# Residual, graph convolution and layer norm in one kernel: a shorter second pass, and the last rows shared and summed in another way

## The reference

```python
masks = (relation[None] == rel_ids[:, None, None, None]).astype(x.dtype)
h = jnp.einsum('rbnm,bmd->rbnd', masks, x)
y = jnp.einsum('rbnd,rdo->bno', h, weight)
x = _layernorm(x + y + bias, axis=-1)          # eps 1e-5
```

## Time and profile before

| | us |
|---|---|
| median of 3 runs (lowest, highest) | 120.71 (120.52, 120.75) |
| the profiled execution, its own time | 120.54 |
| span of the profiled execution, first to last instruction | 118.8 |
| PE busy (matmuls) | 106.6 |
| ACT, DVE, POOL busy | 88.1, 84.8, 70.3 |
| bytes moved | 42.22 MB, mean 355 GB/s |

### The profile page before, as it was taken

The page is one execution under the profiler, slowest core; times in us unless marked ns, Lnnn a source line. Parts: engine busy times, 40 slices in busy tenths (PEclk is TensorE's granted clock), DMA queues, the critical chain, the costliest instruction groups (busy, mean ns, idle before and its releaser), DMA issues.

```text
span 118.8 us, 2879 instructions
## 1 busy us (share of the span) xinstructions
PE 106.6 (90%) x1012; PEld 80.4 (68%) x1023; DVE 84.8 (71%) x252; ACT 88.1 (74%) x114; POOL 70.3 (59%) x132
## 2 busy tenths in 40 slices
PE   6788999899999979999999999999999999999400
PEld 2168898799997646767676767676868676679300
DVE  1055678397877848696959887787779777998840
ACT  4088277947797999799999499968987698925530
POOL 2007001940047998399569955995689577977740
PEclk9999999999999999999999999999999999999985
DMA  3999999999999999999999999999999999450271
GB/s 73 389 408 411 414 407 422 414 391 412 425 414 384 419 403 436 380 414 414 419 391 404 422 406 394 420 406 423 377 433 411 415 399 383 141 177 0 85 248 35
DMA packets 12419, 42.22 MB, mean 355 GB/s; under 512 B 882, under 2 KB 7155, under 8 KB 8947
## 3 DMA queue, kind: packets, MB, share of 16 engines
q1 hardware_dynamic: 12256, 41.49, 88.6%
q10 hardware_dynamic: 146, 0.52, 1.3%
HBM read 37.81 MB, written 4.19 MB: 354 GB/s over the span
## 4 chain that ended last, share of the span: by engine, by line
PE 58%; DMA 29%; SPq 5%; DVE 2%; issue 1%; ACT 0%; DVEq 0%
PE h_ps L619 32%; DMA adj_sb<-adj 29%; PE ids_t L601 16%; PE y_ps L633 9%; SPq L396 4%; PE ids_t L633 1%; DVE x_sb L758 0%; SPq L393 0%; SPq L412 0%; ACT std L539 0%; DVE stats L711 0%; DVE x_sb L705 0%; DVE moments L717 0%; DVEq L255 0%; DVE shift L751 0%
## 5 line engine op out<-in xcount | busy, mean ns | idle before, releaser
L522 ACT ACTIVATE junk<-adj_sb,minus 128x2048 bf16<-128x2048 int32 x32 | 63.8, 1994 | 0.4 <-DMA adj_sb<-adj 0.4
L699 DVE TENSOR_SCALAR mask_t<-ids_t 128x1024 bf16<-128x1024 uint16 x64 | 43.6, 687 | 25.2 <-PE ids_t L601 24.1
L601 PEld LDWEIGHTS ids_t<-ident,adj_sb 128*128 128x128 bf16 x512 | 36.5, 123 | 13.8 <-DMA adj_sb<-adj 2.7
L601 PE MATMUL ids_t<-ident,adj_sb 128*128 128x128 bf16 x512 | 40.0, 221 | 2.3 <-DMA adj_sb<-adj 2.2
L619 PE MATMUL h_ps<-mask_t,x_lo 128*128 128x512 bf16 (+2 forms) x184 | 33.5, 314 | 0.0
L619 PE MATMUL h_ps<-mask_t,x_hi 128*128 128x512 bf16 (+2 forms) x173 | 31.1, 310 | 1.2 <-DVE mask_t L699 0.6
L448 POOL TENSOR_TENSOR x_lo<-x_sb,x_hi 128x1024 f16<-128x1024 f32 x7 | 15.0, 2144 | 24.2 <-ACT x_hi L531 24.2
L488 POOL TENSOR_SCALAR x_sb<-x_sb,rstd,shift 128x128 f32<-128x128 f32 x55 | 24.0, 457 | 1.0
L535 ACT ACTIVATE h_all<-h_ps 128x512 f32<-128x512 f32 (+2 forms) x23 | 10.6, 463 | 18.1 <-PE h_ps L619 18.1
L454 POOL TENSOR_TENSOR x_sb<-x_sb,bias_sb 128x1024 f32<-128x1024 f32 x8 | 19.0, 2377 | 7.8 <-DVE x_lo L764 7.7
L619 PEld LDWEIGHTS h_ps<-mask_t,x_hi 128*128 128x128 f16 x184 | 15.6, 98 | 7.2 <-DVE mask_t L699 1.2
(11 more groups left out here) (44 smaller groups left out, 30.8 us busy)
## 6 DMA issues: line engine op xcount, KB each, us to landing
adj_sb<-adj SPq DMA_DIRECT2D x27, 1024.0 KB, 19.5
adj_sb<-adj SPq DMA_DIRECT2D x10, 512.0 KB, 8.4
x_sb<-x SPq DMA_DIRECT2D x7, 512.0 KB, 18.9
out<-x_sb SPq DMA_DIRECT2D x7, 512.0 KB, 16.7
x_sb<-x ACTq DMA_DIRECT2D x1, 512.0 KB, 5.4
out<-x_sb SPq DMA_DIRECT2D x2, 256.0 KB, 3.3
w_sb<-weight SPq DMA_DIRECT2D x1, 64.0 KB, 6.1
bias_row<-bias ACTq DMA_DIRECT2D x1, 0.5 KB
```

The costliest lines, as they stand in the source:

```text
L522: nc.scalar.activation(junk[:, at % 2], adj_sb[:, slot, 2 * k:2 * k + 2, :], ACT.Square, scale=2.0, bias=minus[:, 0:1], accum_out=squares[ ...
L601: last = nc.tensor.transpose(bank[:, j, :], words[:, j // step(b), j % step(b), 0, :], ident[:, :])
L699: nc.vector.tensor_scalar(mask_t[:, b % 2, :, u * P:(u + 1) * P], ids_t[u % T_BANKS][:, :, :].bitcast(UINT16), 1.0, None, ALU.mult).then_i ...
```

## The change

Four parts.

1. The second pass goes unit by unit instead of batch by batch, with x in fp32 instead of three bf16 parts. The code of one turn gets shorter on every engine; in PE's program it has 44 matmuls instead of 288.
2. PE adds the last unit's x: a matmul of x with an fp32 identity (`add_x`) opens the accumulation that `project(d)` closes. DVE has no sum for d any more: it takes statistics from PSUM and normalises from PSUM.
3. The found matmul stands ahead of `products(d)`, the write of `again` ahead of d's statistics, and `offer_guess(full)` ahead of `find_far`.
4. Rows at the end are shared anew: of full, POOL three and ACT five; of rb, POOL two, DVE two, ACT none. POOL and DVE normalise as (x - mean) * rstd. The shift is only made for full and ra, which ACT still normalises with it.

```diff
+        whole_ident = sb("whole_ident", [P, P], FP32)
...
         def second_pe(pe):
             pe.wait_ge(g_w, 16)
             with pe.Fori(0, B) as b:
...
+                with pe.Fori(0, J) as u:
+                    pe.wait_ge(g_cast, J * b + u + 1)
+                    for j in range(J):
+                        last = nc.tensor.transpose(ids_t[0][:, j, :], ids[:, j, :], ident[:, :])
+                    last.then_inc(g_tr, 1)
+                    pe.wait_ge(g_x, 16 * (b + 1))
+                    pe.wait_ge(g_mask, J * b + u + 1)
+                    for r in range(R):
                         for j in range(J):
+                            last = nc.tensor.matmul(h_ps[0][:, r * P:(r + 1) * P], x_sb[:, 0, j, :], masks[:, r, j, :],
+                                                    start=(j == 0), stop=(j == J - 1))
+                    last.then_inc(g_prod, 1)
+                    pe.wait_ge(g_h, J * b + u + 1)
                     for r in range(R):
+                        last = nc.tensor.matmul(y_ps[:, 0, :], h_all[:, 0, r * P:(r + 1) * P], w_sb[:, r, :],
+                                                start=(r == 0), stop=(r == R - 1))
                     last.then_inc(g_y, 1)
...
             def roots(r):
                 slot = r.b
+                shifted = r.index >= B - 2
...
+                if shifted:
+                    nc.gpsimd.tensor_scalar(minus_mean[:, r.index - (B - 2), r.us], mean[:, slot, r.us], -1.0, None,
+                                            ALU.mult).then_inc(s_minus, 1)
...
-                                        ALU.mult).then_inc(s_root, 1)
-                pool.wait_ge(s_root, r.index + 1)
-                nc.gpsimd.tensor_tensor(shift[:, slot, r.us], minus_mean[:, r.us], rstd[:, slot, r.us],
                                         ALU.mult).then_inc(s_rstd, 1)
+                if shifted:
+
+                    pool.wait_ge(s_rstd, r.index + 1)
+                    pool.wait_ge(s_minus, r.index - (B - 3))
+                    nc.gpsimd.tensor_tensor(shift[:, slot, r.us], minus_mean[:, r.index - (B - 2), r.us], rstd[:, slot, r.us],
+                                            ALU.mult).then_inc(s_shift, 1)
 
             def normalise(r, units):
...
-                    last = nc.gpsimd.tensor_scalar(rows[:, slot, u, :], rows[:, slot, u, :], rstd[:, slot, u:u + 1],
-                                                   shift[:, slot, u:u + 1], ALU.mult, ALU.add)
+                    last = nc.gpsimd.tensor_scalar(rows[:, slot, u, :], rows[:, slot, u, :], mean[:, slot, u:u + 1],
+                                                   rstd[:, slot, u:u + 1], ALU.subtract, ALU.mult)
...
-            normalise(full, full.units[:4])
+            normalise(full, full.units[:3])
             roots(ra)
             normalise(ra, ra.units[:2])
-            normalise(rb, rb.units[:1])
+            normalise(rb, rb.units[:2])
...
             copy_h(c)
-            normalise(full, full.units[4:5])
+            normalise(full, full.units[3:4])
             copy_h(e)
             root(ra)
-            normalise(full, full.units[5:7])
+            normalise(full, full.units[4:6])
             copy_h(d)
-            normalise(full, full.units[7:]).then_inc(s_aside, 1)
+            normalise(full, full.units[6:]).then_inc(s_aside, 1)
             root(rb)
             normalise(ra, ra.units[2:]).then_inc(s_aside, 1)
-            normalise(rb, rb.units[1:2]).then_inc(s_aside, 1)
...
+            def add_x(g):
+
+                pe.wait_ge(s_whole, 1)
+                pe.wait_ge(s_xb, g.b + 1)
+                nc.tensor.matmul(y_of(g)[:, 0, :], whole_ident[:, :], x_sb[:, g.b, g.first, :], start=True, stop=False)
...
             project(c)
-            products(d, 0, 1)
-            project(e)
             pe.wait_ge(s_found, 1)
             nc.tensor.matmul(ids_t[0][0:1, 0, 0:2].bitcast(FP32), found[:, :], ones[:, :],
                              start=True, stop=True).then_inc(s_count, 1)
+            products(d, 0, 1)
+            project(e)
+            add_x(d)
             project(d)
             second_pass(pe, second_pe)
...
+            def statistics_of_sum(g):
+
+                dve.wait_ge(s_y, g.index + 1)
+                nc.vector.bn_stats(stats[:, g.first, :], y_of(g)[:, 0, :]).then_inc(s_st, 1)
...
-                                               in1=guess[:, r.us], op0=ALU.add, op1=ALU.mult).then_inc(s_n[3], 1)
-
-            def shift_rows(r):
...
+                                               in1=guess[:, r.us], op0=ALU.add, op1=ALU.mult).then_inc(s_rstd_last, 1)
...
+            offer_guess(r)
             find_far()
             find()
-            offer_guess(r)
...
-            for g in (e, d):
-                sum_rows(g)
-                statistics(g)
-            combine(rb, d, range(J - 2, J))
+            sum_rows(e)
+            statistics(e)
             dve.wait_ge(s_count, 1)
             nc.vector.tensor_copy(again[:, :], ids_t[0][0:1, 0, 0:2].bitcast(FP32)).then_inc(s_again, 1)
-            for part in (invert, times_guess, times_guess_again, better_guess, shift_rows):
+            statistics_of_sum(d)
+            combine(rb, d, range(J - 2, J))
+            for part in (invert, times_guess, times_guess_again, better_guess):
                 part(rb)
-            normalise(rb, rb.units[2:])
+            normalise(rb, e.first, rows[:, rb.b, e.first, :])
+            normalise(rb, d.first, y_of(d)[:, 0, :]).then_inc(s_done, 1)
```

More of the change, by code:

```diff
@@ L266, in second_sp @@
                 sp.dma_start(x_sb[:, 0], x_v[b]).then_inc(g_x, 16)
-                for k in range(PAIRS):
-                    sp.dma_start(adj_sb[:, 0, 2 * k:2 * k + 2, :], adj_v[b, :, 2 * k:2 * k + 2, :]).then_inc(g_adj[k], 16)
-                for g in range(NG):
-                    sp.wait_ge(g_norm, NG * b + g + 1)
-                    sp.dma_start(out_v[b, :, g * GU:(g + 1) * GU, :], rows[:, 1, g * GU:(g + 1) * GU, :]).then_inc(g_out, 16)
-                sp.wait_ge(g_out, 16 * NG * (b + 1))
@@ L318, in second_pe @@
+                    last.then_inc(g_prod, 1)
+                    pe.wait_ge(g_h, J * b + u + 1)
                     for r in range(R):
-                        done = R * (NG * b + g) + r
-                        pe.wait_ge(g_mask, GU * (done + 1))
-                        if r >= 2:
-                            pe.wait_ge(g_h, done - 1)
-                        for j in range(J):
-                            for n, part in enumerate(parts):
-                                last = nc.tensor.matmul(
-                                    h_ps[r % 2][:, :], part[:, j, :], halves(masks[:, j, :], r % 2),
-                                    start=(j == 0 and n == 0), stop=(j == J - 1 and n == len(parts) - 1))
@@ new lines, in second_dve @@
+            with dve.Fori(0, B * J) as i:
+                dve.wait_ge(g_tr, i + 1)
+                for r in range(R):
+                    last = nc.vector.tensor_scalar(masks[:, r], ids_t[0][:, :, :], float(r + 1), None, ALU.is_equal)
+                last.then_inc(g_mask, 1)
+                dve.wait_ge(g_xb, i + 1)
+                dve.wait_ge(g_y, i + 1)
+                nc.vector.tensor_tensor(result, y_ps[:, 0, :], xb, ALU.add).then_inc(g_sum, 1)
+                dve.wait_ge(g_sum, i + 1)
+                nc.vector.bn_stats(stats[:, 0, :], result).then_inc(g_stats, 1)
+                dve.wait_ge(g_stats, i + 1)
+                nc.vector.memset(square[:, 0:1], 0.0)
+                nc.vector.bn_aggr(moments[:, 0, 0, :], stats[:, 0, :]).then_inc(g_var, 1)
+                dve.wait_ge(g_std, i + 1)
+                nc.vector.reciprocal(guess[:, 0:1], std[:, 0:1]).then_inc(g_root[0], 1)
+                dve.wait_ge(g_root[0], i + 1)
+                nc.vector.scalar_tensor_tensor(out=square[:, 0:1], in0=variance[:, 0, 0:1], scalar=EPS,
+                                               in1=guess[:, 0:1], op0=ALU.add, op1=ALU.mult).then_inc(g_root[1], 1)
+                dve.wait_ge(g_root[1], i + 1)
+                nc.vector.scalar_tensor_tensor(out=whole[:, 0:1], in0=square[:, 0:1], scalar=0.25,
+                                               in1=std[:, 0:1], op0=ALU.mult, op1=ALU.add).then_inc(g_root[2], 1)
+                dve.wait_ge(g_root[2], i + 1)
+                nc.vector.reciprocal(rstd[:, 0, 0:1], whole[:, 0:1]).then_inc(g_root[3], 1)
+                dve.wait_ge(g_root[3], i + 1)
+                nc.vector.tensor_scalar(result, result, mean[:, 0, 0:1], rstd[:, 0, 0:1],
+                                        ALU.subtract, ALU.mult).then_inc(g_norm, 1)
@@ L687, in _ @@
             s_worst = sem("worst_ready")
-            s_n = [sem(f"root{n}") for n in range(4)]
+            s_n = [sem(f"root{n}") for n in range(3)]
             def row_maxima(b):
@@ L746, in better_guess, with normalise @@
                 nc.vector.scalar_tensor_tensor(out=rstd[:, r.b, r.us], in0=twice[:, r.us], scalar=0.75,
[L747 to L760 removed]
```

(5 more changed lines are left out.)

153 lines of the change are left out of this document (38 added, 115 removed).

## The result

The changed kernel is slower: 122.69 us median of four runs, against 120.61 us for the kernel before beside it. The ratio is 1.0163, with a 95% interval of 1.0133 to 1.0193. I had forecast 119.9 us and a range of 119.1 to 120.6. The profiled execution took 122.76 us, its span 121.0. The ratios in this document are those of the comparison itself, not quotients of the medians; one run (one_input's of 123.80 us) was a slow one, and they leave it out.

What follows compares the result with a forecast made beforehand. PE was taken to bound the kernel up to 111.24 us, small row work to 114.21, then the last store, held by a code fetch. Last store -0.95 and POOL last +0.10 made -0.85 us: 119.9 us, range 119.1 to 120.6.

Steps and rivals of the forecast that it cites:

- Against it: both forms read one tile and two scalars: POOL's normalise: argument that the subtract form would not cost over 0.15 us a row more than the old mult/add.
- rival 3: POOL's two last rows, or add_x, cost more; end moves 0.3 to 0.4 us, 121.1 us without fetch gain; chance 0.08.
- the missing shift of sets 0 to 5: Two small POOL operations fewer per set, about 0.5 us, six times; no gain, since PE is the bound there.
- The term of -0.95 us for the last store: End of kernel: shorter jump and earlier flag let the last store land sooner, by 0.64 to 1.45 us, taken as 0.95.
- the jump is short but still starts the fetch of a block: PE's jump at the end: the block only comes earlier, by as much as the flag is read earlier, 0.64 us gained.
- worked out +0.10: Last rows: POOL replaces DVE as the last engine, ending at 114.31, 0.10 us later than the old end.
- My bound of 0.30 us lost: Last rows' worst case: add_x costs 0.47 us and POOL's rows slow to 0.52 us each.
- Rival 1: PE's jump still misses and takes 4 us again; only the earlier flag helps, 120.2 us; chance 0.14.
- Rival 2: Last store's stragglers aren't the fetch's doing and come anyway; only +0.10, 120.8 us, no difference; chance 0.12.

Runs made afterwards that it cites:

- one_input: Changed kernel with DVE's last two search operations written with one input tensor and one scalar column instead of two input tensors; 122.68 us, 1.0107 of before.
- forms: Kernel before with a different form of POOL's normalise (orders of subtract, mult, add) in each of sets 1 to 5; 120.46 us in one run.
- mult_add: Changed kernel with POOL's old normalise (multiply by rstd, add shift) for all sets but the last half's two rows; 120.68 us, 0.997 of before.
- add_mult: Changed kernel with POOL adding minus mean instead of subtracting mean, then multiplying by rstd; 120.64 us, 0.9983 of before.
- stub_pass: Kernel before with the change's second pass, PE's part cut to three matmuls a turn (not the reference's result); 119.28 us, 0.9866 of before.
- four_at_once: shared_as_before with the second pass's products on PE as 8 matmuls instead of 32; 119.05 us, 0.9866 of before.
- shared_as_before: Changed kernel with rows shared and shifted as in the kernel before, POOL using mult/add everywhere; 120.18 us, 0.9941 of before.
- short_pass: Kernel before with only the change's shorter second pass on all five engines; 120.78 us, 1.0007 of before.
- long_pass: shared_as_before with the long second pass of the kernel before; 120.07 us, 0.9928 of before.

## Why the prediction was wrong

- **"Against it: both forms read one tile and two scalars"** is the step that failed. I priced POOL's new rows at the old 0.44 to 0.52 us, and rival 3 had them cost something over 0.15 us more, worth 0.3 to 0.4 us, and only at the end. They cost 0.80 us, because the form has a subtract (forms). The error goes through the whole kernel: 55 rows at 0.35 us are 19 us of POOL's time, and POOL's last row ended at 118.28 us where I had worked out 114.31. I had called the missing shift of sets 0 to 5 "nothing" on the strength of a POOL busy 59%, but never asked what the new form did to the same sets. POOL then had 57.4 of 60 us to do and became the bound; with the subtract gone the loss went (mult_add 0.997, add_mult 0.998 of before). In the kernel before, DVE's two rows with this very form stood at 0.33 us, but no row of POOL did; that was the place for bounds on both sides, and the far one should have been that of an unknown operation, not that of the known one.
- **The term of -0.95 us for the last store** was mis-sized for this change. The reading behind it holds in its main point: a block of PE's code in front of the last store's packets costs 1.5 us by stub_pass, 1.1 us by four_at_once against shared_as_before. What it had wrong is whose block: with the short jump it isn't the one that PE jumps to and waits for. Of the two ways in which I let it go, the second happened: "the jump is short but still starts the fetch of a block". I priced it at 0.64 us, all that the flag is earlier. The block came even 1.05 us earlier, yet it gave 0.2 us in add_mult and nothing in short_pass, where the flag isn't moved. My step was that everything behind the block moves with it. But an earlier block stands before more packets: in shared_as_before it starts before any packet of ra's store, in add_mult after 100 of its 272, and the DMA engine that carries it still has the rest of both stores to do behind it. The packets that come one by one at the end (stub_pass) bear this out; no run took it apart. In the change itself the term came out at 1.8 us, for another reason: POOL's rows were so late that the block, fetched at 116.43 us, was through when the last store was issued at 118.31. That is luck for this term, paid for with the 4.07 us.
- **The rest of the working held.** With the subtract undone, flag, statistics, rstd and both engines' last rows came within 0.1 us of what was worked out, and POOL did take DVE's place as the last (+0.20 us against the old end, worked out +0.10). mult_add and add_mult show no cost of the PSUM source, the matmul with the identity or the new shares beyond that. My bound of 0.30 us lost was a little small: by its own terms it is 0.10 + 0.16 (add_x at 0.47 us, past the CAST's end) + 0.08 = 0.34 us.
- **Rival 1** (the jump still misses) fell: 371 ns. **Rival 2** (the stragglers aren't the fetch's doing) fell as an explanation, though its time, no gain, is what short_pass got. **Rival 3** named the right engine and form, and its condition, over 0.15 us a row, was met; it missed size and place, so its 121.1 us was 1.6 us short.
- **Left open:** why shared_as_before and long_pass are 0.4 us faster in the median than add_mult, though their profiles end in the same way (the sessions differ, shared_as_before's interval overlaps add_mult's and long_pass's just misses it, and the profiled executions, 120.36, 120.26 and 120.27 us, don't show it); why the load of the flag got 0.7 us shorter; whether a border or the jump's length decides; and which of the 16 DMA engines the block takes, which no view shows.

## What to carry to other kernels

An engine that is busy 59% isn't free for a form that it has never run: before an operation is changed in a loop, find a row of that engine with that operation, or measure it, as forms did with five forms in one kernel. When a last store lands late, look for instruction blocks beside its packets: code that is never run can cost time by its length alone, here 1.1 to 1.5 us when the jump's target moved from 2218 or less to 2309 or 2314. And such a block should come before the stores or not at all; moving it a little forward only lets it stand before other packets.

## What the runs showed of the hardware

- A tensor_scalar on GpSimd, 128x128 fp32 with two scalar columns, takes 450 to 452 ns with mult and add in either order, and 794 to 800 ns when either operation is a subtract.
- PE's code comes in blocks of 16 KB through a DMA queue of its own, nine of them (0.15 MB) in the kernel before. Where the rows ended near 114.3 us, one at the wrong moment held the last packets back until 117.5 to 117.8 us; without it they ended between 116.2 and 116.6. That the block shares a DMA engine with them is inferred from this.
- PE's jump over the second pass took 4289 to 4307 ns to a target 677 instructions off, with two blocks fetched after its start; 365 to 371 ns to one 176 off, with one block; and 230 ns to one 26 or 80 off, with none.
- A DVE operation with two input tensors was held for 1.71 us, until GpSimd's two-input add ended; with one input tensor and a scalar column it took 0.21 us beside the same add. The Trainium skill ("GPSIMD Engine Reference", section "Specifications") says that the two engines share SBUF interfaces, with contention from DVE instructions with two SBUF inputs; this agrees.
- PE's sequencer needs 0.1 us for a wait that is already met.
